# Two conditioned attention layers on one core: other orders at the layer change, and a second PSUM bank for one attention

## The reference

```python
xn = layernorm(x) * norm_scale + norm_bias
q, k, v = xn @ Wq + bq, xn @ Wk + bk, xn @ Wv + bv      # 512 x 512 weights each
k = k masked by token; v = 0 on masked tokens
q = softmax(q over the channels of a head); k = softmax(k over the tokens)
att = einsum(k, v)          # one small matrix a head; 16 heads of 32 in layer 0, 8 of 64 in layer 1
y = einsum(q, att)
h = layernorm(y) * (1 + scale(cond)) + shift(cond)
x = x + silu(h) @ Wo + bo
```

## Time and profile before

| | us |
|---|---|
| median of 3 runs | 857.43 (856.22 to 859.86) |
| the profiled execution | 857.14 |
| its span, first to last instruction | 855.1 |
| TensorE busy (share of the span) | 838.2 (98%) |
| VectorE busy | 679.3 (79%) |
| ScalarE busy | 603.1 (71%) |
| GpSimd busy | 548.9 (64%) |

### The profile page before, as it was taken

The page is one execution under the profiler, slowest core; times in us unless marked ns, Lnnn a source line. Parts: engine busy times, 40 slices in busy tenths (PEclk is TensorE's granted clock), DMA queues, the critical chain, the costliest instruction groups (busy, mean ns, idle before and its releaser), DMA issues.

```text
span 855.1 us, 20095 instructions
## 1 busy us (share of the span) xinstructions
PE 838.2 (98%) x6659; PEld 719.9 (84%) x6659; DVE 679.3 (79%) x1362; ACT 603.1 (71%) x1442; POOL 548.9 (64%) x741
## 2 busy tenths in 40 slices
PE   7999999999999999999999999999999999999998
PEld 7778888888888888888878888888888888888886
DVE  6987778778788788778887887787788787787766
ACT  5376687686676776686876886776776686676665
POOL 3467766766766666766767667667667666765641
PEclk9999999999999999999999999999999999999999
DMA  8876676766667756555587556656566656566441
GB/s 309 286 225 201 201 218 199 228 216 205 195 210 208 233 197 199 179 165 175 169 247 233 185 172 200 201 180 201 179 204 201 202 186 189 178 194 211 142 160 62
DMA packets 139404, 169.81 MB, mean 199 GB/s; under 512 B 12302, under 2 KB 112006, under 8 KB 139302
## 3 DMA queue, kind: packets, MB, share of 16 engines
q1 hardware_dynamic: 138512, 167.56, 62.5%
q10 hardware_dynamic: 790, 0.98, 0.4%
HBM read 95.61 MB, written 72.88 MB: 197 GB/s over the span
## 4 chain that ended last, share of the span: by engine, by line
PE 83%; DMA 6%; DVE 4%; issue 2%; SPq 2%; POOL 1%; ACT 1%; DVEq 0%; POOLq 0%; ACTq 0%
PE PS L1152 72%; PE PS L1248 6%; PE PS L1232 3%; DMA X<-in_x 2%; DMA XT<-x_turned 1%; DMA x_turned<-XS 1%; DMA k_turned<-KT 1%; DMA QT<-qy_turned 1%; POOL XL L667 0%; SPq L400 0%; PE PS L1322 0%; DMA EK<-k_turned 0%; DVE BNX L1515 0%; PE PS L1276 0%; PE PS L1291 0%
## 5 line engine op out<-in xcount | busy, mean ns | idle before, releaser
L680 POOL TENSOR_TENSOR HL<-H,HH 128x512 fp32r<-128x512 f32 x60 | 77.5, 1292 | 185.3 <-ACT HH L916 185.3
L867 ACT ACTIVATE Z<-QT,FC,FA 128x128 f32<-128x128 f32 x240 | 99.0, 483 | 87.7 <-DMA QT<-qy_turned 87.7
L1152 PE MATMUL PS<-XH,WH_k 128*128 128x256 f32 x512 | 149.8, 293 | 0.7 <-DVE KN L1581 0.7
L1152 PE MATMUL PS<-XL,WH_k 128*128 128x256 f32 x512 | 144.8, 283 | 0.0
L1152 PE MATMUL PS<-XH,WL_k 128*128 128x256 f32 x512 | 144.8, 283 | 0.0
L953 ACT ACTIVATE XN<-X,NBX,RSX 128x512 f32<-128x512 f32 x60 | 48.8, 813 | 85.5 <-POOL NBX L629 85.5
L829 ACT ACTIVATE SK<-SK,KN 128x128 f32<-128x128 f32 x256 | 98.9, 387 | 10.7 <-DVE KN L1581 10.4
L1152 PE MATMUL PS<-WH_o,HH 128*128 128x512 f32 x248 | 101.3, 408 | 2.0 <-issue 1.9
L1152 PE MATMUL PS<-WH_v,XH 128*128 128x512 f32 x256 | 100.8, 394 | 0.0
L1152 PE MATMUL PS<-WH_q,XH 128*128 128x512 f32 x256 | 100.7, 393 | 0.0
L1152 PE MATMUL PS<-WL_v,XH 128*128 128x512 f32 x256 | 100.3, 392 | 0.0
(11 more groups left out here) (171 smaller groups left out, 2106.6 us busy)
## 6 DMA issues: line engine op xcount, KB each, us to landing
qy_turned<-QS SPq DMA_DIRECT2D x60, 512.0 KB, 2.9
QT<-qy_turned SPq DMA_DIRECT2D x240, 128.0 KB, 3.1
EK<-k_turned SPq DMA_DIRECT2D x128, 128.0 KB, 2.8
x_turned<-XS SPq DMA_DIRECT2D x30, 512.0 KB, 3.3
XT<-x_turned SPq DMA_DIRECT2D x120, 128.0 KB, 3.5
k_turned<-KT SPq DMA_DIRECT2D x52, 256.0 KB, 3.8
out_x<-X SPq DMA_DIRECT2D x31, 256.0 KB, 3.2
X<-in_x SPq DMA_DIRECT2D x11, 512.0 KB, 5.3
```

The lines of the kernel that those rows point to most:

```text
L680: eng.tensor_tensor(hl_of(o), h_of(o), hh_of(o).bitcast(F32), ALU.subtract).then_inc(pool_hl, 1)
L867: z = eng.activation(z_of(o)[:, c * P:c * P + P].rearrange("p (q n) -> p q n", q=Q), src, ACT.Identity, bias=FC[l][:, c, b:b + 1], scale=F ...
L1152: mm = eng.matmul(dst, left[a](c), right[b](c), start=(c == 0 and a + b == 0), stop=(c == C - 1 and a == 1))
```

## The change

Attention 31 gets bank B_TY, with the zeroing of that bank moved to stand ahead of it. On SP some writes, reads and placings of turned data move ahead of weight chunks. On ScalarE two parts of the query weights move ahead of the exponentials of keys 33. On VectorE the statistics of tile 38 move from ahead of the first weight chunk to behind tile 32's values, and those values and a low part of the query weights move ahead of the statistics of 38 to 40. On GpSimd two neighbours change places. TensorE's own list stays as it was: only the bank of attention 31 and its waits differ.

```diff
@@ -282,7 +282,7 @@
-        TOGETHER = [*range(5, B - 3, 2), *range(B + 5, NT - 2, 2)]
+        TOGETHER = [*range(5, B - 3, 2), B - 1, *range(B + 5, NT - 2, 2)]
...
-            return FIRST + sum(a < s for a in FILM_SLOTS[FIRST:]) + (j >= B + 5)
+            return FIRST + sum(a < s for a in FILM_SLOTS[FIRST:]) + (j == B - 1 or j >= B + 5)
@@ -539,38 +539,38 @@
             load_second(eng, 5, [0])
+            write_qy(31)
             load_second(eng, 5, [1])
+            read_qy(31)
             load_second(eng, 5, [2])
-            write_qy(31)
             load_second(eng, 5, [3])
             load_second(eng, 6, [0])
-            read_qy(31)
             write_keys(15)
             load_second(eng, 6, [1])
             write_x(17)
             load_second(eng, 6, [2])
+            load_second(eng, 6, [3])
             place_keys(15)
             load_second_bias(0, dve_v)
             load_second_bias(1, dve_q)
-            load_second(eng, 6, [3])
             load_second_bias(2, pool_bo)
...
             masks_at(32)
-            load_second(eng, 7, [0])
             write_keys(16)
             write_qy(33)
             masks_at(34)
+            place_keys(16)
+            read_qy(33)
+            load_second(eng, 7, [0])
             load_second(eng, 7, [1])
-            read_qy(33)
-            place_keys(16)
             write_qy(34)
             write_x(18)
             read_qy(34)
+            read_x(18)
             load_second(eng, 7, [2])
             load_second(eng, 7, [3])
-            read_x(18)
@@ -780,8 +780,8 @@
             x_low(37)
+            normalise_keys(35)
             mask_of_keys(18)
-            normalise_keys(35)
@@ -1057,11 +1057,11 @@
             exp_k(32)
+            split_high(6, [1])
+            split_high(6, [2])
             exp_k(33)
-            split_high(6, [1])
             norm_y(29)
             heads(30)
-            split_high(6, [2])
             split_high(6, [3])
@@ -1884,13 +1884,12 @@
             stat_x(37)
-            stat_x(38)
             turn_queries(30)
             split_low(eng, 4, [0])
             turn_x(35)
             turn_y(28)
+            keys(31)
             split_low(eng, 4, [2])
-            keys(31)
             split_low(eng, 4, [3])
@@ -1907,16 +1906,18 @@
             keys(33)
+            zero_turned()
             key_sums(32)
             split_low(eng, 6, [0])
+            values(32)
+            split_low(eng, 6, [2])
+            stat_x(38)
             stat_x(39)
             stat_x(40)
             key_sums(33)
             turn_queries(31)
             turn_y(29)
-            split_low(eng, 6, [2])
             mixed(30)
-            values(32)
             queries(32)
...
             second_ones()
-            zero_turned()
             keys(34)
```

## The result

The changed kernel takes 860.24 us as the median of 13 runs (858.25 to 863.36), the kernel before 856.68 us in 13 runs beside them (855.55 to 861.77). The ratio is 1.0034, with a 95% interval of 1.0021 to 1.0048: the change makes the kernel slower by 1.8 to 4.1 us. Ratio and interval come from all the runs, so the ratio is not that of the two medians, which is 1.0042. The profiled execution took 860.24 us, its span is 857.4.

What follows compares the result with a forecast made beforehand. TensorE was taken to bound the kernel, idling 3.8 us at the layer change. Terms reach plus 2.7 at mix 31, minus 1.3 and 0.9 gives plus 0.5: 857.14 becomes 857.6, with 0.3 for the median 857.9; range 855.0 to 861.0.

Steps and rivals of the forecast that it cites:

- rival 2: Values of 32 on VectorE: first bias row takes 7.3 us to land, mix 31 5.3 late, plus 3.1, 860.5; chance 0.23.
- The signs that I named: Predicted profile: keys 32 unwaiting near 420.3, mix 29 waiting 2 us or more, turn_y(29) behind 442, mix 31 waiting for exp_q(31).
- Keys 31 and keys 32: VectorE: KN of tile 31 up to 1.6 us sooner, so TensorE's 0.73 wait at keys 32 goes: minus 0.7.
- The read ahead of two chunks: SP queue: tile 31's reads hold back chunks 2 and 3 of the values' weight; mix 29 at 429.1, plus 2.2.
- Attention 31's bank: TensorE: attention 31 no longer waits for heads(30), mix 30 still does; minus 0.4.
- VectorE and the bias row: VectorE, 434 to 443 us: added work and 0.4 bias wait end turn_y(29) at 442.7; plus 1.7 more at mix 31.
- the shorter way: Second path to mix 31, through mixed(30), root_y(30), x_low(34) and x_turned(35): ScalarE free for exp_q(31) at 449.6.
- keys 16: Earlier placing on SP: attention 32 no longer waits, 1.3 us of delay gone.
- Keys 17: GpSimd makes tile 35's keys 0.7 sooner, ahead of a mask; attention 34's wait of 0.90 is used up: minus 0.9.
- the first (gains arrive): Whole layer change: new waits short, mix 31 late by 1 us or less; minus 1.2, 856.2; chance 0.22.

Runs made afterwards that it cites:

- c_part_back: Changed kernel with tile 31's read put back, VectorE's two transposes moved first, and the query weight's last chunk behind two bias rows again; ratio 0.9998.
- u_read31: Changed kernel with one edit undone: on SP the write and reads of tile 31 again behind the values' weight chunks; ratio 1.0026.
- a_values_back: Changed kernel with one VectorE call put back: the values of tile 32 behind mixed(30) again; ratio 1.0021.
- u_dve: Changed kernel with VectorE's list as before the change, except the zeroing, which stays ahead; ratio 1.0013.
- a_fill: Changed kernel with eight extra 128x128 products, no part of the computation, in TensorE's idle time ahead of mix 29; ratio 1.0038.
- o_read31: Kernel before with one edit alone: write and reads of tile 31 ahead of chunks 2 and 3 of the values' weight; ratio 1.0046.
- before_again: The kernel before measured once more with no edit; ratio 0.9989.
- o_values: Kernel before with only tile 32's values and a query weight low part moved ahead of the statistics of 39 and 40 on VectorE; ratio 1.0021.
- o_place: Kernel before with only keys 16's placing and the read of x 18 ahead of output weight chunks, and keys 35 ahead of the mask; ratio 0.9982.
- o_bank: Kernel before with the bank edit alone: attention 31 in the other bank, its zeroing ahead; ratio 0.9993.

## Why the prediction was right, and where it was too small

The time went the way of the forecast, by more: I said plus 0.5, measured are plus 1.8 to 4.1, and the median 860.24 lies inside the range. It does not lie in the part around the forecast (856.7 to 859.1) to which I gave 0.50, but next to the 860.5 of rival 2, and not by rival 2's way. The signs that I named came: keys 32 at 420.19 without a wait, the stall at mix 29, `turn_y(29)` behind 442, mix 31 waiting for `exp_q(31)`, attentions 32 and 34 without a wait. The 0.5% (4.3 us) that I took for what can be told from no change was too wide; the interval of the result is some 0.13% to each side. Step by step:

*Keys 31 and keys 32*: right, KN of 31 ends at 419.93 and the wait of 0.73 is gone. c_part_back and u_read31 show what it is worth at the end: nothing, since output 28 waits for h 28. I gave the later low parts slack because TensorE needs them late, and overlooked that SP's chunk 2 waits for one of them; in the changed kernel this costs nothing, in the three kernels with the read put back it does.

*The read ahead of two chunks*: right in place and size. Reads at 422.63 (forecast 422.85), chunks at 424.43 (424.7), the chunk was used 3.2 us later, as I took it, mix 29 at 428.84 (429.1), 1.4 late. That was the good end: the traces of the four other kernels with this read had ScalarE's third part behind idles of 4.35 to 4.94 us (a_values_back, u_dve, a_fill, o_read31) and mix 29 late by 2.4 to 3.4. The sum took 3.2 us, near the short end of the 2.8 to 4.7 that the prediction allowed, for a transfer that took 3.1 to 4.7. The estimate of 2.6 us by the Trainium skill (DMA: Bandwidth & Descriptors, Anatomy of one DMA) is below all of them, the shortest being 3.1 us; for this queue with its reads in flight the measurement decides.

*Attention 31's bank*: right, 0.5 us at mix 30 where nothing else is changed, and it doesn't arrive.

*The step that was missing*: at mix 30 I had plus 1.0, measured is plus 2.3. The sum priced an idle TensorE by its length only. Mix 29 and output 27 ran at half clock, and took from 428.84 to 434.21, 5.4 us, where from 427.58 to 431.24 they had 3.7. a_fill shows the link: with work in the idle time the clock doesn't fall, and 1.7 us between the mixes are not lost. The times of all runs bear it out. The mean granted clock of a run is 0.9963 for the changed kernel and 0.9951 to 0.9969 for the six experiments whose trace has a stall of over 2 us at mix 29 or 31. It is 0.9974 over the 94 runs of the kernel before, and 0.9975 to 0.9980 for the six others.

*VectorE and the bias row*: right in kind. The values wait 0.32 us in the changed kernel (I had 0.4; the first landing of a bias row is 4.3 us behind the issue at 433.95), and 2.15 and 2.26 where nothing else delays VectorE. `turn_y(29)` ends at 443.94 and not at 442.7: KN of 33 is 1.2 later than I had it, since `film(28)` started at 430.75 (430.1; ScalarE waited 0.95 us for a chunk of the query weight) and the addition of output 27 waited 0.63 for a TensorE at half clock. The write then landed in 2.6 us (I took 3.4), and what I called the shorter way came in as late as the other: `root_y(30)`, `x_low(34)` at 447.16 (445.9), `x_turned(35)` at 448.56 behind an idle of 3.49, and from there ScalarE works without idle until `exp_q(31)` at 450.92. The last read of tile 32, issued at 447.9, took 2.9 us, so it was there at about 450.8. Mix 31 is 3.4 late and not 2.7.

*What is absorbed*: keys 16 give back 0.8 us (I had 1.3), because mix 32 has a new idle of 0.48 us. Keys 17 give back 1.0 (0.9). So mix 34 is 1.6 late, and attention 34 stands at 490.09.

That leaves about 1.3 us between the trace's layer change (1.6) and the measured 2.9. The trace shows 0.9 more from mix 34 to the end, where the orders are the same; before_again shows 1.5 there with no edit at all. I can't tell these from scatter.

*The rivals*: the first (gains arrive) is out. The second had the right place; the bias row didn't need 7.3 us to decide, 4.3 were enough, because SP issued it at 433.95 and not at 432.6. The two causes don't add up: with either one taken out the other keeps mix 31 from 3.7 to 4.6 late (u_dve, u_read31), and the time at or above that of the kernel before. Only with both out is the ratio 1 (1.0001 and 0.9998), and u_dve's interval reaches 1.0000 too.

## What to carry to other kernels

In a list that an engine takes strictly in order, look at each moved instruction's wait and name what stands behind it on that engine and on the engine that it feeds: a read moved up ahead of three weight chunks held the SP queue for 3.8 us (418.83 to 422.63), and through the next chunk the copy that TensorE waited for. When two causes hold one instruction, undo them together before judging either: with one alone taken out, mix 31 stayed 3.7 to 4.6 us late. Look, too, at what an undone edit meets in the rest of the change: here `write_qy(31)` came back behind a chunk that the moved keys 31 had made late. And price a stall of TensorE of 2 us with the slow stretch behind it, not by its length alone.

## What the hardware showed that I had not expected

Behind an idle of 2.09 us (mix 29) the granted clock was 0.50 in the window 430 to 432, behind 2.15 us (u_read31, mix 31) 0.50 in 452 to 454, each time with TensorE busy throughout; it had been 1.00 until the idle. It fell to 0.50 as well behind 2.13 us (o_values), 2.14 (a_fill, mix 31), 2.62 (c_part_back, output 28), 2.64 (u_dve), 3.04 (a_values_back) and 3.20 (o_read31). Behind 1.59 (o_place), 1.62 (o_bank), 1.65 (a_fill), 1.71 and 1.72 us (u_read31) it stayed at 1.00. In u_dve and a_values_back it fell 0.1 and 0.8 us before TensorE had work again. A 128x512 product starts every 0.23 us at the full clock and every 0.43 at the half. The Trainium skill (TensorE: Matmul & The Clock Gate, Part 1: The HAM clock gate) knows only these two levels, 1.2 and 2.4 GHz; the rows agree, values between them stand only in windows in which the clock changes. The cost is not in the idle row: at mix 29 it was 2.09 us of idle and another 1.7 of slow work, which later waits hid in part.
